# Graph layer and expert mixture on one core: products of the experts' first stage placed in two steps, and another order in the tiles of the first block

## The reference

```python
grouped = x.reshape(B, S // t, t, D)                       # groups of t = 16 rows
cont_logits = jnp.einsum('bgtd,des->bgtes', grouped, controller)
cont_perm = (cont_logits == max over the 16 rows)          # one row of a group for each of 16 x 4 (e, s)
intermediate = jnp.einsum('bgtd,desf->bgtesf', grouped, f1)
inner = relu(jnp.einsum('bgtesf,bgtes->bgesf', intermediate, cont_perm))
inter2 = jnp.einsum('bgesf,esfd->bgesd', inner, f2)        # f is 32 wide, d is 512
result = jnp.einsum('bgesd,bgtes->bgtd', inter2, cont_perm)
```

## Time and profile before

| | |
|---|---|
| median of three runs | 2024.03 us (2021.88 to 2025.5) |
| the profiled execution, its own time | 2019.68 us |
| its span, first to last instruction | 2018.0 us |
| PE busy | 1857.1 us (92%) |
| PEld busy | 1362.2 us (68%) |
| DVE busy | 1190.3 us (59%) |
| ACT busy | 988.5 us (49%) |
| POOL busy | 364.5 us (18%) |
| share of PE in the chain that ended last | 39%, with "issue" 3% |

### The profile page before, as it was taken

How to read it: one execution, slowest core, us unless ns; L and a number is a source line. 1 busy time by engine, 2 the same in 40 slices (tenths; PEclk the granted TensorE clock), 3 DMA queues, 4 the chain that set the end, 5 groups by cost and what they waited for, 6 DMA issues and landing times. The chain is left out here.

```text
span 2018.0 us, 41277 instructions
## 1 busy us (share of the span) xinstructions
PE 1857.1 (92%) x15896; PEld 1362.2 (68%) x15896; DVE 1190.3 (59%) x2345; ACT 988.5 (49%) x1716; POOL 364.5 (18%) x428
## 2 busy tenths in 40 slices
PE   5486899999999899999999879998998989999998
PEld 3354678888888788888888765565655656665654
DVE  6487566666666444333333366676766767667655
ACT  2254223333333386566556255565655657556543
POOL 4486310000000000000000052222222222222210
PEclk9688899999999999999999999999999999999999
DMA  9977756665556364344333263443434434344322
GB/s 368 306 147 106 200 142 183 180 178 164 162 167 190 123 263 155 122 141 164 122 133 131 92 225 114 127 134 105 151 115 128 127 106 158 113 131 137 107 75 69
DMA packets 162435, 305.68 MB, mean 151 GB/s; under 512 B 15506, under 2 KB 87186, under 8 KB 159091
## 3 DMA queue, kind: packets, MB, share of 16 engines
q1 hardware_dynamic: 153327, 282.66, 43.8%
q0 software_dynamic: 8960, 20.98, 5.3%
HBM read 168.72 MB, written 134.87 MB: 150 GB/s over the span
## 5 line engine op out<-in xcount | busy, mean ns | idle before, releaser
L1488 PE MATMUL bank<-f2s,inner_bd 128*32 128x512 f32 x2528 | 300.5, 601 | 6.9 <-issue 6.3
L1372 ACT ACTIVATE inter_hi<-bank 128x512 fp32r<-128x512 f32 x316 | 188.9, 598 | 201.7 <-PE bank L1488 199.9
L598 ACT ACTIVATE h1o<-bank,b_by_channel 128x500 f32<-128x500 f32 x160 | 108.5, 678 | 324.8 <-PE bank L430 316.3
L1294 DVE TENSOR_TENSOR inter_lo<-bank,inter_hi 128x512 fp32r<-128x512 f32 x316 | 216.1, 689 | 84.8 <-ACT inter_hi L1372 83.2
L428 PE MATMUL bank<-hhi,w_hi 128*128 128x500 f32 x624 | 244.7, 392 | 0.0
L430 PE MATMUL bank<-hhi,w_lo 128*128 128x500 f32 x624 | 243.6, 390 | 0.0
L429 PE MATMUL bank<-hlo,w_hi 128*128 128x500 f32 x624 | 242.6, 389 | 0.0
L428 PE MATMUL bank<-ahi,w_hi 128*128 128x500 f32 x608 | 237.3, 390 | 0.0
L429 PE MATMUL bank<-alo,w_hi 128*128 128x500 f32 x608 | 236.6, 389 | 0.0
L430 PE MATMUL bank<-ahi,w_lo 128*128 128x500 f32 x608 | 236.4, 389 | 0.0
L562 DVE BATCH_NORM_STATS2 stats<-h1o 128x500 f32 (+1 forms) x160 | 103.2, 674 | 155.6 <-ACT h1o L598 155.6
(11 more groups left out here) (149 smaller groups left out, 3356.9 us busy)
## 6 DMA issues: line engine op xcount, KB each, us to landing
h1T<-h1o SPq DMA_DIRECT2D x19, 2000.0 KB, 8.0
h1in<-h1T SPq DMA_DIRECT2D x19, 2000.0 KB, 9.7
aggregate<-at SPq DMA_DIRECT2D x20, 1024.0 KB
x<-in_x SPq DMA_DIRECT2D x79, 256.0 KB, 2.6
x<-x SPq DMA_DIRECT2D x79, 256.0 KB, 3.7
x_back<-x SPq DMA_DIRECT2D x79, 256.0 KB, 2.8
out<-x_back SPq DMA_DIRECT2D x79, 256.0 KB, 2.1
h2in<-h2T SPq DMA_DIRECT2D x39, 512.0 KB, 4.0
```

The costliest lines, as they stand in the source:

```text
L598: nc.scalar.activation(h1o[b][:, m, :], mb[m % 4][:, 0:CW], ACT.Identity, bias=b1c[:, m:m + 1]).then_inc(evr, 1)
L1294: nc.vector.tensor_tensor(ilo[u % QB][:, :], bI[u % QB][:, :], ihi[u % QB][:, :].bitcast(F32), ALU.subtract).then_inc(ilr, 1)
L1372: nc.scalar.activation(ihi[n % QB][:, :], bI[n % QB][:, :], ACT.Copy).then_inc(ihr, 1)
L1488: last = nc.tensor.matmul(bI[b][32 * i:32 * i + 32, :], ibd[:, e, j, :, :].rearrange("p s g -> p (s g)"), f2s[:, e, :], start=True, stop=True)
```

## The change

At the block's end, for k = 1 to 9 (nine of the ten places), the last step of a back block becomes: rows, sums, then three of the four units in the order of quarters 2, 3, 0, norm, `inner` 0, the unit of quarter 1, turn_g, `inner` 1, turn_x, logits and select, `inner` 2, final. Step 0 of the next block keeps only `inner` 3, between its first two units. Bank bD[1] now serves `inner` 1 alone, and quarters 0, 2 and 3 share bD[0]. `final` of the last step waits for the relu of `inner` 1, since it writes bD[1]. The units' waits follow the new order of quarters. At k = 9 the front has only seven tiles, so its last step has neither sums nor turn_x nor logits. The first place (before step 0 of k = 1) stays as it was, as `inner` 0 at the end of the front-only block.

In front-only tiles (block 0), `spread` comes after the new tile's turn_g and stats. The silus of a pair come whole in an even tile, before the spread and before the copies of `sums`.

```diff
+        bQ = [bD[0], bD[1], bD[0], bD[0]]
...
+        def crossing(kb, j):
+            return kb is not None and kb < NB - 1 and j == tiles(kb) - 1
+        def quarters(kb, j):
+            return (2, 3, 0, 1) if crossing(kb, j) else (0, 1, 2, 3)
...
-                if ahead and m % 2 == 0:
+                if ahead and behind and m % 2 == 0:
                     yield "spread", m // 2
...
-                if behind and m == 0:
-                    yield "inner", 1
+                if crossing(back, m):
+                    if ahead:
+                        yield "sums", m
+                    for p in range(3):
+                        yield "unit", u + p
+                        yield "low", u + p
+                    if next_:
+                        yield "norm", m + 2
+                    yield "inner", (front, 0)
+                    yield "unit", u + 3
+                    yield "low", u + 3
+                    if new:
+                        yield "turn_g", m + 3
+                        yield "stats", m + 3
+                    yield "inner", (front, 1)
+                    if next_:
+                        yield "turn_x", m + 2
+                elif behind and m == 0 and back > 0:
+                    yield "unit", u
+                    yield "low", u
+                    if next_:
+                        yield "norm", m + 2
+                    yield "inner", (back, 3)
+                    yield "unit", u + 1
+                    yield "low", u + 1
+                    if new:
+                        yield "turn_g", m + 3
+                    yield "unit", u + 2
+                    yield "low", u + 2
+                    if new:
+                        yield "stats", m + 3
+                    yield "unit", u + 3
+                    yield "low", u + 3
+                    if ahead:
+                        yield "sums", m
+                    if next_:
+                        yield "turn_x", m + 2
...
                     if new:
                         yield "turn_g", m + 3
                         yield "stats", m + 3
+                    if m % 2 == 0:
+                        if exists(front, m + 4):
+                            yield "silu", ((m + 4) // 2, 0 if m else KH // 2, KH)
+                        yield "spread", m // 2
                     yield "warm", 3
...
-                if exists(front, m + 4 + m % 2):
+                if exists(front, m + 4 + m % 2) and (behind or m == TB - 1):
                     yield "silu", ((m + 4 + m % 2) // 2, (1 - m % 2) * KH // 2, (2 - m % 2) * KH // 2)
+                if crossing(back, m):
+                    yield "inner", (front, 2)
                 if behind:
                     yield "final", m
                     yield "result", m
-            if front is not None:
-                yield "inner", 0
+            if front is not None and back is None:
+                yield "inner", (front, 0)
...
                     pe.wait_ge(yr, min((k * TB + j) * KH + 2, NT * KH) if k is not None else NT * KH)
+                    if crossing(kb, j):
+                        pe.wait_ge(inv, (k * QB + 2) * 2)
+                        pe.wait_ge(ina, (k * QB + 2) * 2)
```

More of the change, by code:

```diff
@@ L958, in pair_size, with quarter, lows @@
             return 2 if exists(k, 2 * p + 1) else 1
+        def crossing(kb, j):
+            return kb is not None and kb < NB - 1 and j == tiles(kb) - 1
+        def quarters(kb, j):
+            return (2, 3, 0, 1) if crossing(kb, j) else (0, 1, 2, 3)
+        def quarter(kb, u):
+            return quarters(kb, u // QB)[u % QB]
+        def lows(kb, j, b):
+            kb, j = (kb, j) if j >= 0 else (kb - 1, tiles(kb - 1) - 1)
+            return unit_of(kb, j * QB + quarters(kb, j).index(b)) + 1
         def schedule(front, back):
@@ L999, in schedule @@
                     yield "keep", m // 2
-                if behind and m == 0:
-                    yield "inner", 1
+                if crossing(back, m):
[35 more added lines that the diff above has]
+                        yield "turn_x", m + 2
+                elif behind and m == 0:
+                    yield "inner", (back, 1)
                     yield "unit", u
@@ L1007, in schedule @@
                         yield "turn_g", m + 3
-                    yield "inner", 2
+                    yield "inner", (back, 2)
                     yield "unit", u + 1
@@ L1012, in schedule @@
                         yield "stats", m + 3
-                    yield "inner", 3
+                    yield "inner", (back, 3)
                     yield "unit", u + 2
@@ L1070, in schedule @@
                     yield "result", m
-            if front is not None:
-                yield "inner", 0
+            if front is not None and back is None:
+                yield "inner", (front, 0)
         def relu(op, q, s, *more):
             return op(ibd[32 * s:32 * s + 32, QE * q:QE * q + QE, :, s, :],
-                      bD[q % 2][32 * s:32 * s + 32, 0:QE * TB * GB].rearrange("p (e j g) -> p e j g", e=QE, g=GB), *more)
+                      bQ[q][32 * s:32 * s + 32, 0:QE * TB * GB].rearrange("p (e j g) -> p e j g", e=QE, g=GB), *more)
         def unit_of(kb, u):
             return kb * UNITS + u
-        def block_of(q, k, kb):
-            return k if q == 0 else kb
         with nc.Block() as block:
@@ L1328, in body @@
                         if what == "inner":
-                            dve.wait_ge(inp, block_of(n, k, kb) * QB + n + 1)
-                            if static(block_of(n, k, kb), 1) and n == 0:
+                            dve.wait_ge(inp, n[0] * QB + n[1] + 1)
+                            if static(n[0], 1) and n[1] == 0:
                                 dve.wait_ge(ibz, PIECES)
                             for s in range(0, NS, 2):
-                                relu(nc.vector.tensor_scalar_max, n, s, 0.0).then_inc(inv, 1)
+                                relu(nc.vector.tensor_scalar_max, n[1], s, 0.0).then_inc(inv, 1)
                 blocks(dve, body)
@@ L1380, in body @@
                         if what == "inner":
-                            act.wait_ge(inp, block_of(n, k, kb) * QB + n + 1)
-                            if static(block_of(n, k, kb), 1) and n == 0:
+                            act.wait_ge(inp, n[0] * QB + n[1] + 1)
+                            if static(n[0], 1) and n[1] == 0:
                                 act.wait_ge(ibz, PIECES)
                             for s in range(1, NS, 2):
-                                relu(nc.scalar.activation, n, s, ACT.Relu).then_inc(ina, 1)
+                                relu(nc.scalar.activation, n[1], s, ACT.Relu).then_inc(ina, 1)
                 blocks(act, body)
@@ L1445, in sums @@
                         if h and kb is not None:
-                            pe.wait_ge(ilr, unit_of(kb, j * QB + 1) + 1)
+                            pe.wait_ge(ilr, lows(kb, j - 1 if crossing(kb, j) else j, 1))
                         done = {}
@@ L1473, in inter @@
                 def inter(k, kb, u):
-                    j, b, q = u // QB, u % QB, unit_of(kb, u)
+                    j, b, q = u // QB, quarter(kb, u), unit_of(kb, u)
                     if b < 2:
-                        pe.wait_ge(yr, (k * TB + j if k is not None else NT) * KH)
+                        done = NT if k is None else min(k * TB + j + 1, k * TB + tiles(k)) if crossing(kb, j) else k * TB + j
+                        pe.wait_ge(yr, done * KH)
                     if static(kb, 1) and u == 0:
@@ L1484, in inter @@
                     if not static(q, QB):
-                        pe.wait_ge(ilr, q - QB + 1)
+                        pe.wait_ge(ilr, lows(kb, j - 1, b))
                     for i in range(NS):
@@ L1509, in inner @@
                         pe.wait_ge(yr, (k * TB + tiles(k)) * KH)
[L1510 to L1515, removed]
+                    if q == 1 and not static(k, 1):
+                        pe.wait_ge(otr, k * TB - 1)
+                    if q >= 2:
+                        last = 0 if q == 2 else 2
+                        pe.wait_ge(inv, (k * QB + last + 1) * 2)
+                        pe.wait_ge(ina, (k * QB + last + 1) * 2)
                     for e in range(QE * q, QE * q + QE):
@@ L1551, in body @@
                         if what == "inner":
-                            inner(block_of(n, k, kb), n)
+                            inner(*n)
                 blocks(pe, body)
```

16 lines of the change are left out of this document (8 added, 8 removed).

## The result

The changed kernel takes 1994.06 us (median of four runs, 1990.86 to 1996.08) against 2023.73 for the kernel before on the same chip: a ratio of 0.9852 with a 95% interval of 0.9834 to 0.9870. That is about 30 us faster. The prediction was 2013 with a range of 2000 to 2026: the direction was right, and the gain was 2.7 times the forecast (29.7 us for 11).

The account below looks back on a forecast made before the run. The prediction took TensorE's own idle time, stops for instruction refills, to bound the kernel. Refills -22, new waits +4.6 and +8.8, and front-only block -3 made -11.6, rounded to -11: 2013 us from 2024.0, range 2000 to 2026.

Parts of the forecast that it names:

- the refills' period: TensorE's stops inside quarters: instruction buffer refilled every 256 instructions, about 3.7 us from one resumption to the next.
- the sum of -11.6: Whole kernel: refills -22, new waits +4.6 and +8.8, front-only block -3, rounded to -11.
- fourth rival: Quarters: idle time is no refill and stays, +10, 2034 us; chance 0.13 together with the third rival.
- third rival: Quarters 0 to 2: last step's 256 KB transfers delay fetches, +24, 2048 us; chance 0.13 together with the fourth rival.
- T: Refill time on TensorE, from one resumption to the next, about 3.7 us; longer when transfers are in the way.
- Part 1: Refills at nine places between blocks: idle falls from 36.8 to 15 us, -22, bounds -31 to -10.
- late fetches: Quarters 0 to 2: refills delayed by the last step's 256 KB transfers, put at 4 us.
- Part 2: Crossing's new data waits at eight places: sums on the previous result +4.6, logits on turn_x's copy +8.8; bounds 0 to 16.
- the copies into yT come just in time: Last step's third unit: ScalarE's four copies finish as it needs their banks, wait taken as 0 (0 to 0.3 each).
- D: Time in which TensorE executes a block of 256 instructions; a refill's idle time is the refill time less this.
- Part 3: Front-only block: silu -1.6, selection -0.9, late spread +1.7 per pair, four pairs -3; bounds -10.6 to +4.
- second rival: Whole kernel: refills almost always meet the new waits and are short, -29 + 11 - 6 = -24, 2000 us; chance 0.10.

Follow-up runs that it names:

- shifted: Kernel before with eight more warm matmuls on the identity (16 in the trace, 32 instructions) at the mixture's start; 2021.83 us, one execution.
- half_quarters: Kernel before with two of the four input chunks in each quarter's product, leaving out half of f1; 1945.64 us, one execution.
- load_late: Kernel before with the 512 KB load of step 0 issued one step later, behind step 1's first transfer; 2008.72 us, ratio 0.9948.
- unit_ahead: Changed kernel with the first unit of the crossing step ahead of its sums; 1997.35 us, ratio 0.9887 against the kernel before.
- turn_ahead: Changed kernel with the crossing step's turn_x ahead of quarter 1, not behind it; 1992.09 us, ratio 0.9863 against the kernel before.
- spread_first: Changed kernel with the spread back at the start of an even front-only tile, silus still early; 1989.44 us, ratio 0.9854 against the kernel before.

## Why the prediction was wrong

**What bounds it, and the refills' period.** Right. The stops are refills of 256 instructions, shown by shifted and half_quarters. (Between the second and the third stop of the earlier trace rows lie 105 + 8 + 14 = 127 matmuls, not 128, and the sum of -11.6 rounds to -12; neither matters.) My fourth rival, that they are no refills, is out, and with it what a buffer of 2048 instructions would mean. The third rival (T = 5.7 on quarters 0 to 2) did not come: at the nine places only seven stops were left.

**Part 1, the refills: -22 predicted, about -40 measured.** This is the step that failed, as a size. I kept 15 us of idle time where 6.5 were left, and I put at nothing what a stop costs beside the idle time in its row. The places lost 28.4 us although 3.9 and 7.2 us of new waits came in, so the refills gave 28.4 + 11.1 = 39.5. It has three terms.

- *Idle in the rows*: from 36.8 to 6.5 (9.5 less 3.0 of the first place), so -30.3 where I had -22. Of the 15 that I had kept, 8 were for eight places, 2.7 for the ninth and 4 for late fetches; the rows have 4.4 in the eight and 2.1 in the ninth, and at none of these stops had the 256 instructions before it taken over 4.2 us. So the 4 us for late fetches did not come about, and half of the 8 did not either.
- *The clock*: I left it out. Behind the longest stops it falls to its lower level while PE works on. The "0.98 to 1.00" ahead of the prediction is the mean of long stretches and hides it. In the kernel before, around the third place:

```profile
1390.00:1393.00 3.00, 0.39 (x12) 0.30 (x16) 0.01 (x1) 0.01 (x1) 0.38 (x1) 1.00 0.05 16
1393.00:1397.00 4.00, 4.00 (x28) 1.42 (x22) 1.97 (x4) 1.94 (x4) 0.00 (x0) 0.57 0.02 4
1397.00:1400.00 3.00, 2.65 (x19) 2.06 (x18) 0.24 (x1) 2.90 (x7) 1.89 (x2) 1.00 0.00 0
```

and the timeline of TensorE behind that stop:

```profile
1392.74 3.10 PE L1488 MATMUL bank<-f2s,inner_bd 128*32 128x512 f32 x16
```

  Two units take 3.10 us for 1.9 behind the stop of 3.55 us. The trace before has three such spells of 3.41 us from 1210 us on, none of them in the changed kernel: up to 3 x 3.41 / 2 = 5 us, all of it counted as busy. All three follow late refills (6.3, 5.7 and 6.0 us), and load_late, where none is over 5.2, has one such spell.
- *Idle that shows as busy*: about 4 us, what is left of 39.5. A matmul's record is longer than its share of the pipeline: in the kernel before, the last of 23 matmuls before a stop starts at 1218.05 + 22 x 0.015 = 1218.38 and the next one at 1219.07. That is 0.69 us, and the row says 0.49 idle.

```profile
1218.05 0.54 PE L1520 MATMUL bank<-yT,f1s 128*32 128x64 f32 x23
```

  The same reading at all 27 stops inside a quarter, from 1210 us on, gives 0.21 each time. With 0.2 hidden in each stop, and 28 stops at the nine places before against 7 after, that is 4 us. Behind a unit even more can hide: in the changed kernel eight matmuls of a unit are recorded with 2.18 us at 1388.05, where eight take 1.06, with no idle time at all.

**Part 2, the new waits: +13.4 predicted, +11.1 in the rows.** Right in place and near in size: 0.48 for 0.55 and 0.9 for 1.1, each eight times. That the copies into yT come just in time was right as well (no wait of a unit for them), and unit_ahead shows that there were not 0.9 us to spare. That the wait of logits is counted in D was right in part: 3 of 7 us came back as stops in turn_ahead.

**Part 3, the front-only block: -3 predicted, +3.3 measured.** Here too the clock is the step that failed; the waits came out nearly as said. The silus' waits went (-6.4, as forecast). The selection's fell by 2.3 where I had 0.9 for each of four pairs, and those of sums rose by 7.4, from 1.2 to 8.6, where I had 1.7 for each pair: three are 1.76 long, and the first is 3.3, since `constants` stands in DVE's queue there too. That is -1.3 for -3. But behind these waits came the lower clock, which I had not counted: 4.5 us more of busy time. spread_first shows that the early silus alone would have given the 3 us and more (3.6).

**The sum.** -39.5 + 11.1 + 3.3 = -25.1, the mixture's -25.3. The start of the mixture is 1.7 later in this execution. The page's busy time of TensorE agrees with the parts: 5 of clock and 4 of hidden idle less at the places, 4.5 of clock more in the front, and it fell by 4.9. The two profiled executions are thus 23.6 apart, and the medians 30: the one before, at 2019.68, was faster than all four beside the result, and the one after was the slowest of its four. The rest I put down to this scatter; the medians of the kernel before, 2018.9 to 2023.7 in the four comparisons, show it as well. My second rival (-24, a chance of 0.10) came nearest. Its -29 for idle time and +11 for the waits are what the rows show; its -6 for the front-only block is wrong, and it leaves out the clock and the hidden idle time as I did, so that its total is near by luck in part.

## What to carry to other kernels

When an engine stops in the middle of a run of equal instructions with no releaser, count the instructions from stop to stop. If the distance is constant, suspect that the engine is short of instructions, and test it by putting some in ahead. Then spread dense stretches of small instructions between long ones, and keep large transfers away from them. Idle time in rows is a lower bound of what such stops cost, since a stop can also drag the clock down and hides in part in long records. And a step that is moved behind others in order to fill one gap should be checked for who waits for it: here the late spread cost more than the gap that it filled.

## What the runs showed of the hardware

- TensorE's instructions come in blocks of 16.4 KB, one packet for 256 instructions. In the kernel before it takes 3.4 us from one resumption to the next at least and mostly 3.5 to 4.7 us; five times it takes 5.3 to 6.3 us, with 0.8 to 1.1 MB of other transfers under way. An instruction stream with 128 matmuls of 64 columns and their weight loads in 1.92 us outruns it twofold.
- The Trainium skill's page "Runtime: NRT & Kernel Launch", section "Instruction fetch mechanics", says that the next block is fetched while the current one runs and that this is hidden. By the first, all runs agree; by the second, half_quarters nearly agrees (2.2 us of stops), and the kernel before does not (40 us of stops).
- The granted clock fell to its lower level (1.2 GHz) for 3.4 us behind the stops of 2.96, 3.26 and 3.55 us in the kernel before, not behind one of 2.79. In the front-only tiles of the changed kernel it fell behind the wait of 3.3 us and two of the three of 1.8. Stops of 1 to 2.5 us in load_late left it at the upper level but once.
